# A routed graph-and-FFN layer on one core: router scores from the raw sum, a gather by matmuls, and the last pass combined on chip

## The reference

```python
x = x + gnn(layernorm(x), edges) + mix(layernorm(x))        # this is x2
xl = layernorm(x)
logits = xl @ Wr + br                                       # 8 experts
top_p, top_i = top_k(softmax(logits), 2)
h = relu(xl @ W1[e] + b1[e]); y = h @ W2[e] + b2[e]         # W1: 1024x2048, W2: 2048x1024
out = x + sum over the token's two experts of top_p * y
```

## Time and profile before

| | us |
|---|---|
| median of 3 runs (1150.87 to 1151.68) | 1151.53 |
| the profiled execution | 1149.6 |
| its span, first to last instruction | 1147.9 |

### The profile page before, as it was taken

One profiled execution on the slowest core, in us unless ns is written; L12 is line 12 of the kernel. 1 busy time (PEld: TensorE's weight loads), 2 busy tenths in 40 slices (PEclk: granted clock), 3 DMA queues, 4 the chain that ended last, 5 costly groups with the idle time before them and its releaser, 6 DMA issues.

```text
span 1147.9 us, 14944 instructions
## 1 busy us (share of the span) xinstructions
PE 1032.1 (90%) x5160; PEld 890.2 (78%) x5160; DVE 803.3 (70%) x1106; ACT 625.7 (55%) x793; POOL 128.8 (11%) x182
## 2 busy tenths in 40 slices
PE   4999999999999988788799619999999999999991
PEld 3899999988888987676588517888878788787881
DVE  6357777847668663777633536887888888788875
ACT  4367777432312322666622406777777777777771
POOL 2011323310100001233300020000000000000002
PEclk9999999999999988667899658999999999999996
DMA  8633223265354433000033336999999999999996
GB/s 302 185 115 110 80 87 107 87 187 174 111 165 134 124 112 108 1 1 1 0 131 131 110 128 235 353 377 358 370 390 359 377 363 381 361 376 388 345 378 238
DMA packets 118775, 239.37 MB, mean 209 GB/s; under 512 B 7068, under 2 KB 24220, under 8 KB 116164
## 3 DMA queue, kind: packets, MB, share of 16 engines
q1 hardware_dynamic: 113620, 226.96, 57.2%
q0 software_dynamic: 1760, 6.37, 1.5%
q10 hardware_dynamic: 3344, 5.39, 1.3%
HBM read 211.81 MB, written 26.89 MB: 208 GB/s over the span
## 4 chain that ended last, share of the span: by engine, by line
PE 64%; issue 18%; DVE 8%; ACT 4%; POOL 3%; DMA 2%; POOLq 0%; SPq 0%; DVEq 0%; ACTq 0%
PE bank L1116 30%; PE bank L858 6%; PE bank L860 6%; PE bank L859 6%; PE bank L871 2%; PE bank L873 2%; PE bank L872 2%; PE bank L987 2%; DVE dense L1434 2%; ACT dense L752 2%; DVE dense L1425 1%; PE bank L1027 1%; PE bank L1103 1%; PE bank L929 1%; PE bank L945 1%
## 5 line engine op out<-in xcount | busy, mean ns | idle before, releaser
L1475 DVE TENSOR_TENSOR wlo<-raw,whi 128x2048 fp32r<-128x2048 f32 x74 | 169.3, 2289 | 30.9 <-ACT whi L780 30.1
L780 ACT ACTIVATE whi<-raw 128x2048 fp32r<-128x2048 f32 x74 | 141.6, 1915 | 49.8 <-DMA raw<-in_wffn 21.1
L1170 DVE TENSOR_TENSOR wlo<-raw,whi 128x1024 fp32r<-128x1024 f32 (+1 forms) x72 | 116.4, 1621 | 67.9 <-ACT whi L587 67.2
L587 ACT ACTIVATE whi<-raw 128x1024 fp32r<-128x1024 f32 (+1 forms) x72 | 89.1, 1242 | 137.3 <-PE bank L873 72.0
L780 ACT ACTIVATE a_all<-raw 128x2048 fp32r<-128x2048 f32 x73 | 139.9, 1916 | 39.0 <-DMA raw<-in_wffn 19.3
L1475 DVE TENSOR_TENSOR t_all<-raw,a_all 128x2048 fp32r<-128x2048 f32 x36 | 82.6, 2293 | 40.3 <-ACT a_all L780 40.3
L858 PE MATMUL bank<-a_all,whi 128*128 128x384 f32 x320 | 108.6, 339 | 0.0
L860 PE MATMUL bank<-a_all,wlo 128*128 128x384 f32 x320 | 107.1, 335 | 0.0
L859 PE MATMUL bank<-a_all,whi 128*128 128x384 f32 x320 | 107.0, 334 | 0.0
L1116 PE MATMUL bank<-a_all,xg 128*128 128x512 f32 x360 | 105.2, 406 | 0.0
L1116 PE MATMUL bank<-whi,t_all 128*128 128x512 f32 x288 | 100.7, 411 | 0.0
(11 more groups left out here) (249 smaller groups left out, 2107.6 us busy)
## 6 DMA issues: line engine op xcount, KB each, us to landing
raw<-in_wffn SPq DMA_DIRECT2D x152, 512.0 KB
raw<-in_wffn SPq DMA_DIRECT2D x72, 1024.0 KB
raw<-in_wall SPq DMA_DIRECT2D x28, 1024.0 KB
yrows<-zero SPq DMA_DIRECT2D x33, 512.0 KB, 6.7
raw<-in_wall SPq DMA_DIRECT2D x32, 512.0 KB
dense<-yrows SPq DMA_DIRECT2D x9, 512.0 KB, 7.9
yrows<-dense ACTq DMA_DIRECT2D x18, 256.0 KB, 5.8
x_tok<-in_x SPq DMA_DIRECT2D x3, 512.0 KB, 4.3
```

The source lines that it names most:

```text
L587: act.activation(ring(whi, k), part(k), ACT.Copy).then_inc(hi_done, width(k))
L780: act.activation(hi_ring[u % RAW], raw[:, u % RAW, :], ACT.Copy).then_inc(hi_done, 2)
L1170: dve.tensor_tensor(ring(wlo, k), part(k), ring(whi, k).bitcast(F32), ALU.subtract).then_inc(lo_done, width(k))
L1475: dve.tensor_tensor(lo_ring[u % RAW], raw[:, u % RAW, :], hi_ring[u % RAW].bitcast(F32), ALU.subtract)\
```

## The change

1. **Scores from x2.** With mean m and inverse deviation r of a token, the score is r · (x2 · Wr − m · colsum(Wr)) + br. The column sums come from eight small matmuls early in the layers. The first half of x2 is transposed after the sixth of the last eight pieces and its scores are added up after the seventh; the second half follows as its tiles are added. `bn_stats` runs on each half when it is there. The normalisation of x2 moves to ACT, beside the routing. The square root's table is loaded ahead. Unit 0 of the experts is split earlier.
2. **Routing.** The softmax leaves the path: the top two are taken from the scores, and weights, the busiest expert and `over` are computed after pass 0's tokens are split. Ranks get the base of their expert in the rank matmul itself. Each expert has C = 384 rows in HBM, so a token's row no longer depends on the busiest expert.
3. **Pass 0's tokens** are gathered by 24 matmuls of xl with a one-hot matrix `hot0`. The scatters stay, for the later passes.
4. **The last pass** (the busiest expert's second 128 tokens) stands outside the loop, behind the branch on `over`. Its y isn't stored: six matmuls with a weighted one-hot matrix (`backT`) bring its rows to their tokens. The rows of the other passes, now in `y_dram`, are gathered during it. VectorE adds them, then the six results; the output goes out in six transfers.

```diff
@@ SP: zeros, slots and the last pass
-                if 0 <= z < TURNS * ZERO_BLOCKS:
+                if 0 <= z < NE * C // P:
...
+                elif NE * C // P <= z < NE * C // P + NE:
...
+                    sp.dma_start(y_dram[e * C + SLOTS:(e + 1) * C, :].rearrange("(p r) (a n) -> p (r a) n", p=P, a=8),
...
-                    if u == UNITS // 2:
+                    if u == UNITS // 2 and row is not None:
                         sp.wait_ge(x_turned, 2 * g + 2)
-                        sp.dma_start(x_slot, rows[bass.ds((g + 1) * SLOTS, SLOTS), :]).then_inc(x_in, 16)
+                        sp.wait_ge(scattered, 16 * 2 * NT)
+                        sp.dma_start(x_slot, rows[bass.ds(row, SLOTS), :]).then_inc(x_in, 16)
...
+            expert(more * MORE + NE, busiest, None, None)
@@ POOL
             pool.wait_ge(routed, 1)
+            pool.wait_ge(xl_ready, NT)
...
-            with pool.Fori(0, PASSES) as g:
+            with pool.Fori(0, NE) as g:
                 expert(g, g)
+            pool.wait_ge(busy_ready, 4)
             more = pool.value_load(over[0:1, 0:1], min_val=0, max_val=1)
...
-            pool.wait_ge(y_all, 1)
+            pool.wait_ge(last_turn, 1)
+            pool.tensor_copy(pick[:, :], picks[:, NE:NE + 1].to_broadcast([P, P])).then_inc(pick_ready, 1)
+            pool.wait_ge(g_out, 1)
@@ ACT: router and last pass
+            act.wait_ge(used, LAYER_PIECES - 2 + SPLIT)
+            hi_f(0, 0)
+            act.activation(small[:, 156:157], ident[:, 0:1], ACT.Sqrt)
+            for c in range(KT // 2, KT):
+                x2_copy(c)
             act.wait_ge(var_ready, 2)
             act.activation(small[:, 8:8 + NT], small[:, 4:4 + NT], ACT.Sqrt).then_inc(std_ready, 1)
...
+            hi_f(0, 1)
+            act.wait_ge(nm_ready, 1)
+            for t in range(NT):
+                act.activation(mo_t[:, t, :], x_tok[:, t, :], ACT.Identity, bias=small[:, 148 + t:149 + t], scale=small[:, t:t + 1]).then_inc(xl_ready, 1)
+            hi_f(0, 2)
...
+                    if row is None and u == 8:
+                        act.wait_ge(y_in, g * 32 + 32)
+                        act.wait_ge(g_turned, 1)
+                        act.activation(backT, bank[6][:, 0:N].rearrange("p (t n) -> p t n", t=NT), ACT.Copy).then_inc(g_out, 1)
@@ PE: column sums, scores, gather, last pass
+                    for j in range(KT):
+                        last = pe.matmul(bank[5][:, 0:NE], ones32, wr_sb[:, j, :], start=(j == 0), stop=(j == KT - 1))
+                    last.then_inc(csum_full, 1)
...
+                if m == 5:
+                    pe.wait_ge(x2_added, NT)
+                    turn_x2(range(KT // 2), range(NT))
...
+                if m == 6:
+                    score(range(KT // 2))
+            for t in range(NT):
+                pe.wait_ge(x2_added, NT + t + 1)
+                turn_x2(range(KT // 2, KT), (t,))
+            score(range(KT // 2, KT)).then_inc(logits, 1)
...
+            pe.wait_ge(hot0_ready, 1)
+            pe.wait_ge(xl_ready, NT)
+            for j in range(2):
+                for k in range(4):
+                    for t in range(NT):
+                        last = pe.matmul(bank[6 + j][:, k * P:(k + 1) * P], mo_t[:, t, (4 * j + k) * P:(4 * j + k + 1) * P], hot0[:, t, :],
+                                         start=(t == 0), stop=(t == NT - 1))
+                last.then_inc(x_turned, 1)
...
+            def combine(g, i):
+                pe.wait_ge(y_copied, 2 * g + i + 3)
+                for t in range(NT):
+                    pe.matmul(bank[(0, 1, 4, 5, 6, 7)[NT * i + t]][:, :], backT[:, t, :], y_row[:, i * 512:(i + 1) * 512],
+                              start=True, stop=True).then_inc(comb_full, 1)
...
+                if final:
+                    pe.wait_ge(biased, g + 1)
+                    pe.sem_inc(last_turn, 1)
                 pe.wait_ge(pick_ready, g + 1)
+                if final:
+                    pe.wait_ge(g_ready, 1)
+                    for t in range(NT):
+                        last = pe.transpose(bank[6][:, t * P:(t + 1) * P], back[:, t, :], ident[:, :])
+                    last.then_inc(g_turned, 1)
...
+                        if i == 1 and q == 1 and final:
+                            pe.wait_ge(g_out, 1)
+                            combine(g, 0)
+                if final:
+                    combine(g, 1)
...
-            with pe.Fori(0, PASSES) as g:
-                expert(g)
+            with pe.Fori(0, NE) as g:
+                expert(g, False)
...
             with pe.If(more > 0):
...
+            expert(more * MORE + NE, True)
@@ DVE: routing
...
+            link(dve.scalar_tensor_tensor(out=one[:, 0, :], in0=rk[:, :, 0], scalar=1.0, in1=sel16[:, :, 0], op0=ALU.add, op1=ALU.mult))
+            for t in range(NT):
+                last = dve.tensor_scalar(hot0[:, t, :], slot1[:, :], one[:, 0, t:t + 1], None, ALU.is_equal)
+            last.then_inc(hot0_ready, 1)
...
             dve.tensor_copy(posi[:, :, :], posf).then_inc(routed, 1)
-            dve.wait_ge(routed, 1)
+            lo_f(0, 1)
+            lo_f(0, 2)
...
             x_low(0)
+            dve.tensor_tensor(cen, srt, srt[:, :, 0:1].to_broadcast([P, NT, NE]), ALU.subtract).then_inc(cent, 1)
...
+            for o in range(2):
+                for t in range(NT):
+                    dve.wait_ge(comb_full, NT * o + t + 1)
+                    r = x_tok[:, t, o * 512:(o + 1) * 512]
+                    dve.tensor_tensor(r, bank[(0, 1, 4, 5, 6, 7)[NT * o + t]][:, :], r, ALU.add).then_inc(fin, 1)
```

More of the change, by code:

```diff
@@ L770, in _, with x2_copy @@
             act.activation(A_hi[:, 0:KT // 2, :], moT[:, 0:KT // 2, :], ACT.Copy).then_inc(mo_hi, 1)
-            for k in starts[starts.index(OUT):]:
-                for n in ahead(k):
-                    hi(n)
+            def x2_copy(c):
+                act.wait_ge(x2_turned, c + 1)
+                act.activation(dense[:, c, :], bank[(0, 1, 3, 7)[c % 4]][:, 0:N], ACT.Copy).then_inc(x2_out, 1)
             def hi_f(g, u):
@@ L1467, in _ @@
                         r = x_tok[:, t, o * 512:(o + 1) * 512]
[L1468 to L1479 removed]
+                        dve.tensor_tensor(r, bank[BANKS * o + t][:, :], r, ALU.add).then_inc(x2_added, 1)
@@ new lines, in _ @@
+                    dve.wait_ge(x2_added, NT * o + NT)
+                    for t in range(NT):
+                        last = dve.bn_stats(st[:, t, o, :], x_tok[:, t, o * 512:(o + 1) * 512])
+                if k == LAYER_PIECES - 4:
+                    lo_f(0, 0)
+            link(last)
+            inverse_std(1)
+            negr, nmr = small[:, 144:144 + NT], small[:, 148:148 + NT]
+            link(dve.tensor_scalar(negr, small[:, 0:NT], -1.0, None, ALU.mult))
+            dve.tensor_tensor(nmr, mv[:, :, 0], negr, ALU.mult).then_inc(nm_ready, 1)
@@ L1504, in _ @@
-            rk = gp_bank("rank", 0)[:, 0:NT * NE].rearrange("p (t e) -> p t e", t=NT)
-            cnt = gp_bank("rank", 0)[:, NT * NE:(NT + 1) * NE]
-            cnt_s, top, owner, shift = (busy[:, i, :] for i in range(4))
-            link(dve.tensor_copy(cnt_s, cnt))
-            link(dve.max(top, cnt_s))
-            link(dve.max_index(busy_i[:, :], top, cnt_s))
-            link(dve.tensor_copy(extra[:, :], busy_i[:, 0:1]))
-            link(dve.tensor_copy(small[:, 62:63], busy_i[:, 0:1]))
@@ new lines, in _ @@
+            cnt_s, top, owner = (busy[:, i, :] for i in range(3))
+            link(dve.tensor_copy(cnt_s, cnt))
+            link(dve.max(top, cnt_s))
+            link(dve.max_index(busy_i[:, :], top, cnt_s))
+            link(dve.tensor_copy(small[:, 62:63], busy_i[:, 0:1]))
+            dve.tensor_copy(extra[:, :], busy_i[:, 0:1]).then_inc(busy_ready, 1)
+            link(dve.tensor_scalar(owner, eid[:, :], small[:, 62:63], None, ALU.is_equal))
+            link(dve.tensor_tensor(top, owner, picks[:, 0:NE], ALU.mult))
@@ new lines, in _ @@
+            link(dve.tensor_tensor(w8, wgt, is8, ALU.mult))
+            link(dve.tensor_tensor(wgt, wgt, w8, ALU.subtract))
+            link(dve.tensor_tensor(w8[:, 0, :], w8[:, 0, :], w8[:, 1, :], ALU.add))
+            link(dve.tensor_tensor(val[:, 0, :], val[:, 0, :], val[:, 1, :], ALU.add))
+            for t in range(NT):
+                last = dve.tensor_scalar(back[:, t, :], slot1[:, :], val[:, 0, t:t + 1], w8[:, 0, t:t + 1], ALU.is_equal, ALU.mult)
+            last.then_inc(g_ready, 1)
```

356 lines of the change are left out of this document (197 added, 159 removed).

## The result

| | before | changed |
|---|---|---|
| median (lowest to highest), us | 1151.2 (1150.39 to 1151.68) | 1118.83 (1116.87 to 1119.98) |
| ratio, 95% interval | | 0.9718 (0.9701 to 0.9735) |
| profiled execution; its span | 1149.6; 1147.9 | 1119.98; 1118.2 |

The change wins 32 us. The forecast was 1111.1 in a range of 1103 to 1121. Sign and range hold. The point is 7.7 us too low, on the figure of rival 1 (1119), and the time lies just outside the forecast's own range without the rivals, 1105 to 1118. Put on the profile, the span is 10.7 us over the forecast's 1107.5. The rows say where.

What follows compares the result with a forecast made beforehand. TensorE was taken as the bound, with winnable time only at router and end. Front 30.4 plus last pass and tail 10.0 gave 40.4 us less: span 1107.5, median 1111.1; own range 1105 to 1118, with rivals 1103 to 1121.

Steps and rivals of the forecast that it cites:

- rival 1: Last pass becomes DMA-bound: gathers delay units 14 and 15 and VectorE's adds, returning 8 of 10 us: 1119; chance 0.13.
- The front: From the last layer to the last pass's start: pass 0 starts at 662.0, and 30.4 us are won.
- POOL's queue: Before pass 0: six scatters, then the pick, end later than the token split at 659.8; bounds 659.3 to 666.2, taken 662.0.
- the start nearer 666: Pass 0's start if VectorE's hold on the shared port shuts out POOL's descriptor writing; 659.8 without that rule.
- Pass 0 at full clock: Pass 0 runs at full clock from its start, not half clock at first: 2.6 us less.
- The gap before the last pass: TensorE idles before the last pass for its branch and POOL's pick: 3.0 us taken, bounds 0.3 and 5.
- The step that failed: At the last pass's branch, ACT, VectorE and SP hide theirs behind 4 us of split units; a far-target fetch rule adds 2.
- signs of being wrong: Pass 0 after 668, period over 48.3, TensorE waiting on splits in the last pass, or adds over 5 us late.
- The gathers' term: Gathering the other passes' rows during the last pass and adding them costs 1.5 us, bounds 0 and 6.
- the end: Last pass and tail take 61.5 us instead of 71.5, so 10.0 us are won.
- Rival 3: Passes lose their code: loop-back branches stall TensorE, 7 × 7.5 = 52 us more, time 1164; chance 0.02.
- Rival 4: The extra passes are taken: 17 × 48 us more, near 1927; chance under 0.01.

Runs made afterwards that it cites:

- run 12: The changed kernel measured again, on the chip of two combined follow-up kernels: 1118.05 us, ratio 0.9726.
- run 9: Changed kernel with POOL's pick for pass 0 copied before its six scatters instead of behind them: 1114.13 us, ratio 0.9672.
- run 4: Changed kernel with pass 0's tokens scattered, loaded and transposed as before, new scores and routing kept: 1134.47 us, ratio 0.9861.
- run 10: Changed kernel with the early POOL pick and three of VectorE's weighted adds before the split of unit 15: 1112.82 us, ratio 0.9666.
- run 11: Changed kernel with early pick, three early adds, and the last pass laid out right behind the branch on TensorE, ACT and SP: 1120.80 us, ratio 0.9733.
- run 5: Changed kernel with the extra passes' code left out on TensorE alone: 1115.13 us, ratio 0.9680.
- run 1: Changed kernel with the extra passes' code left out on all five engines: 1111.14 us, ratio 0.9659.
- run 7: Changed kernel with the last pass laid out right behind the branch on TensorE, ACT and SP, extra passes jumped over afterwards: 1119.86 us, ratio 0.9724.
- Run 8: Changed kernel with three of VectorE's six weighted adds put before its split of unit 15: 1116.22 us, ratio 0.9701.
- run 2: Changed kernel without the six late gathers, so their sums are missing from the output: 1111.58 us, ratio 0.9647.

## Why the prediction was right, and where it was not

**The front: right.** The forecast had the last layer matmul at 641.8, `posi` at 651.3, the gather at 7.6 us, pass 0 at 662.0. Measured: 643.6, 653.1, 8.2 and 663.7; in run 12 the first is 642.2 and pass 0 starts at 662.2. These 1.4 us come and go between executions of the same program. TensorE waits 2.0 us for VectorE at 217 us in both, and behind it the clock falls in one and not in the other (the changed kernel, then run 12):

```profile
216.00:222.00 6.00, 4.93 (x19) 4.93 (x20) 5.91 (x11) 0.47 (x1) 2.40 (x20) 0.72 0.84 272
```

```profile
216.00:222.00 6.00, 4.92 (x28) 4.92 (x29) 5.91 (x11) 0.48 (x1) 2.41 (x20) 1.00 0.89 271
```

POOL's queue was the last link before pass 0, as forecast, and run 9 shows it: with the pick ahead of the scatters the idle time fell by 1.5 us. From `posi` to pass 0 it took 10.6 us where the forecast had 10.7, but that is partly luck: the forecast's own terms (scatters of 7.4 us, four of them slowed by 0.6, a pick of 1.45, from 651.6 on) add up to 662.9, not 662.0. The forecast had four scatters slowed by 0.6 and a slow pick; it was two scatters slowed by 1.90 and 0.85 and a pick at its fastest, since VectorE was not at a large split then. The Trainium skill (SBUF — State Buffer, "SBUF: two separate sides") says that VectorE, while it holds the port pair that the two share, shuts POOL out from writing its descriptors. The trace agrees for the two scatters that lie beside VectorE's splits, and the start nearer 666 that the rule alone would give did not come. What is shown of the front is this: pass 0 starts 26.1 us earlier than before, and run 4 puts 11.3 of them down to the gather by matmuls. No run takes the new scores or the new routing out alone; the other 14.8 us are read from the timelines.

**Pass 0 at full clock: not right.** The clock was 0.59 from 664 to 668. TensorE had idled from 660.7 to 663.7. With 1.50 us of idle time (runs 9, 10 and 11) the clock stayed whole, and in runs 9 and 10 the eight passes took 385.0 and 384.9 us, not 385.8. So the clock cost 0.9 us of the 1.8 that the forecast's 384.0 is short, and the rest is open.

**The gap before the last pass: right**, 2.6 for 3.0, and run 5 shows that TensorE's own jump is its cause. The branch ended 1.8 us behind pass 7, exactly as worked out; POOL's pick then took 0.29 us, not 1.45.

**The step that failed** is the sentence "ACT, VectorE and SP have up to 4 us of split units in hand and hide theirs behind it". ACT reaches its branch only after it has stored pass 7's y, 3 us after that pass's end, and then stands up to 7.2 us: 10.7 us from the end of one split to the start of the next, more than the 4 in hand. The last pass took 54.9 us where 50.0 were forecast: TensorE waited 2.1 us for h at 1064.19, and over 1066 to 1070 its granted clock was 0.81, where run 1 has 1.00. TensorE waiting in the last pass was one of the forecast's own signs of being wrong, and it came. SP's jump came earlier (1044.6) and its own share was not measured apart from ACT's. The Trainium skill (Runtime: NRT & Kernel Launch, "Instruction fetch mechanics") says that a taken branch to a far target must fetch first. The trace agrees for TensorE, ACT and SP, and run 7, where the target lies right behind the branch, has ACT's next instruction after 0.1 us. The prediction weighed that rule for SP and gave it 2 us; it did not put ACT's own position in the program beside it. VectorE went on 0.2 us after its branch, so the price is not the same on each engine.

**The gathers' term, 1.5 us, was too small.** The fetches of units 14 and 15 came late, and the six adds stood behind the late split; from the last matmul to the end it took 11.2 us, not 8.5. Run 8 takes 3.8 of these away, and run 2 has 6.8. The six adds themselves were sized rightly (3.92 + 3.93 for 7.7), and so were a combine of three matmuls (2.74 and 2.84 for 2.6), the out transfer, and the passes of 48.0.

So the front gave 26.9 us of the 30.4, the end 2.8 of the 10.0 (71.5 → 68.7). That the time still fell inside the stated range is owed to the room that rival 1 gave it, and rival 1 had the right time with its mechanism as half of the cause: runs 1 and 2 show that it takes the late jumps and the gathers together, and that either one removed gives 7 us back. Rival 3 did not come: none of the passes lost its code. Rival 4 neither.

## What to carry to other kernels

Before a branch is moved ahead of the work that it used to follow, find for each engine the instruction that it reaches the branch with, and the buffers that are in hand at that moment: the engine that comes to it last has the least left to hide the jump behind. Two losses that draw on the same slack must be priced together; each looked free or cheap here when it was priced alone, and taking either out was worth 7 us while the other was there. A short operation that the next stage waits for goes ahead of a queue of long ones, not behind it.

## What was not expected of the hardware

- The next instruction after a taken branch over the extra passes came after 4.0 to 6.2 us on TensorE (4.9 in the changed kernel), 4.2 to 5.8 on SP, 4.0 to 7.2 on ACT (in nine executions), and 0.2 on VectorE. Where the branch fell through to code right behind it, ACT needed 0.1.
- After the gather, the granted clock fell inside pass 0 in all nine profiled executions in which TensorE idled 2.9 to 3.6 us before it (0.59 from 664 to 668 in the changed kernel). In the three with 1.50 us of idle time it stayed at 1.00. After a wait of 2.0 us at 217 us it fell in some executions and not in others.
- The same code laid out in another order made eight passes 4 to 5 us longer, in two kernels.
